# Loading three batches ahead of scales and weights, and the second half of batch 0 ahead of batch 2's statistics

## The chip, the cores and the metric

The kernel runs on one core of one Trainium2 chip. The metric is the device time of one execution in microseconds (us), as the median of several runs. TensorE (PE) does the matmuls and transposes, VectorE (DVE), ScalarE (ACT) and GpSimd (POOL) the elementwise work. SyncE (SP) issues nearly all loads and stores of the stretch that is changed here.

## The reference

For 16 batches of a 128x1024 tile `x` and a 128x256 tile `ctx`: a layer norm, a cross attention with a skip path, a second layer norm and a feed-forward network with 4-bit weights.

```python
n = layernorm(x)                                   # rows of 1024
q, k, v = Wq @ n, Wk @ ctx, Wv @ ctx
energy = einsum('bcn,bcm->bnm', q, k) / sqrt(C)    # C = 128
x = x + Wskip @ n + einsum('bnm,bcm->bcn', softmax(energy), v)
n = layernorm(x)
h = silu(n @ dequantize(gate).T) * (n @ dequantize(up).T)
x = x + h @ dequantize(down).T                     # inter = 2752, groups of 64
```

## The kernel before, in words

The work has two stages. The attention stage (the first 230 us or so) takes the 16 batches in `STEPS = 17` steps, one batch to a step, and writes the split, transposed activations to `xt`. The feed-forward stage that follows is a long run of matmuls (10 pairs of weight tiles in a hardware loop, and a remainder), for which DVE and ACT unpack the weights.

Each engine has its own program written out by hand, and each works strictly in the order of that program. Semaphores are the only tie between engines. So the order of the calls in `step(i)` of ACT, in `step(i, meanwhile)` of DVE and in SyncE's list of loads is the order in which things happen.

One batch is worked on in two halves, `f = 0` and `f = 1`, of 512 of the 1024 columns:

- DVE computes mean and variance of the batch's rows (`row_stats`: `BN_STATS` twice, `BN_AGGR` once), POOL makes the inverse deviation (`inverse_deviation`), DVE writes the normalised rows (`normalize(0, b)`, into `xn`).
- PE multiplies ctx by the fused query-key matrix and the value matrix (`keys_values(b)`, semaphore `s_kv`). ACT copies the keys to `kk` (`keys_out`) and the values to `v_t` (`values_out`).
- PE computes the energies of a half (`energies(b, f)`), DVE their row maxima (`maxima(b, f)`), ACT the exponentials with their sums (`exponentials`), DVE the inverse of the sums (`inverse_total`), ACT the scaled probabilities (`normalize_probs`). PE transposes them (`probs_transposed`), ACT copies them out (`probs_out`), PE multiplies by the values (`values(b, f)`), and DVE adds the result to the batch's row (`add_attention`).

In step `i` PE does `energies(i, 0)`, `values(i-1, 0)`, `energies(i, 1)`, `probs_transposed(i-1, 1)`, `keys_values(i+1)`, `values(i-1, 1)`, `probs_transposed(i, 0)`, with transposes of the second layer norm's blocks between them. `energies(i, 0)` needs `kk` of batch i, which ACT writes in step i-1.

SyncE's list in `before` begins with ctx and x of batches 0 and 1, then the six arrays of scales and zeros for all weights (172 KB each; DVE's `extremes` takes their maxima at the end of step 0, POOL reduces them over the partitions, and `powers_of_two` uses that in step 2), then the packed weights and the scale grid of the first weight tile (`load_raw(0, 0)`, `load_grid(0, 0)`; used from step 4 on), and then, for each further batch, its ctx and x. A load of batch i >= 2 waits for `s_kv >= i-1`, since ctx has two buffers; from batch 5 on it waits for the store of batch i-5 too.

In `before`, DVE's step 0 reads (L1056 is `inverse_total`, L1019 and L1023 are `row_stats`, L1041 is `maxima`, L981 is `extremes`):

```python
maxima(0, 0); inverse_total(0, 0)
x_arrived(2); row_stats(0, 2)      # waits for x of batch 2
maxima(0, 1)
extremes()                         # waits for scales and zeros
inverse_total(0, 1)
```

ACT's step 0 is `exponentials(0, 0)`, `normalize_probs(0, 0)`, `exponentials(0, 1)`, `keys_out(1)`, `normalize_probs(0, 1)`, `values_out(1)`, `probs_out(0, 0)`; L706 is an exponential, L720 a `normalize_probs`, L691 `keys_out`, L695 `values_out`, L701 `probs_out`. On PE L434 is `energies`, L422 `probs_transposed`, L462 and L467 are the skip part and the value part of `values`.

Of the kernel before, what the change touches and what calls it, by code (L numbers as in the profile page):

```python
# [15 lines left out]
B, C, N = 16, 128, 1024  # L16
# [29 lines left out]
def batch_of(i):  # L46

    return 8 * (i // 8) + i % 8 // 2 + 4 * (i % 2)
# [39 lines left out]
def build(nc, x, ctx_in, att_weights, packed, grids, scales, zeros, out):  # L88
    ctx = ExitStack()
    with ctx:  # L90
# [3 lines left out]
        def sem(name):  # L94
            return ctx.enter_context(nc.semaphore(name))
# [19 lines left out]
        grids_all = w_gu0[:, :, :, :].rearrange("p a o n -> p (a o n)")[:, 0:12 * 344].bitcast(F32).rearrange(  # L115
            "p (k n) -> p k n", k=6)
# [45 lines left out]
        s_grids_in = sem("s_grids_in")  # L162
# [75 lines left out]
        def wait(eng, s, count):  # L238
            if not isinstance(count, int) or count > 0:
                eng.wait_ge(s, count)  # L240

        @block.sync
        def _(sp):
            def load_batch(i):
                k, par = i // 2, i % 2
                if i >= 2:
                    sp.wait_ge(s_x_in[par], 16 * k)
                    wait(sp, s_kv, i - 1)
                if i >= XROWS:
                    sp.wait_ge(s_xn2, i - XROWS + 1)  # L250
                    sp.wait_ge(s_store[i % XROWS], 16 * (i // XROWS))
                b = batch_of(i)
                sp.dma_start(ctx_sb[:, par, :], ctx_in[b, :, :]).then_inc(s_ctx_in[par], 16)
                sp.dma_start(row(i), x[b, :, :]).then_inc(s_x_in[par], 16)

            def store_batch(i):
                sp.wait_ge(s_res, 2 * i + 2)
                sp.dma_start(out[batch_of(i), :, :], row(i)).then_inc(s_store[i % XROWS], 16)

            def load_grid(job, done):  # L260
                wait(sp, s_weight, done)
                for g in range(QG):
                    rows = slice(g * P // QG, (g + 1) * P // QG)
                    sp.dma_start(grid[rows, :, :], grids[job, g:g + 1, :, :].to_broadcast([P // QG, 2, JW])
                                 ).then_inc(s_grid_in, 16)

            def load_raw(job, done):
                wait(sp, s_weight_lo, done)
                sp.dma_start(raw[:, :], packed[job, :, :]).then_inc(s_raw_in, 16)

            def load_raw_d(job, done):
                wait(sp, s_weight_lo, done)
                sp.dma_start(raw_d[:, :], packed[job, :, :]).then_inc(s_raw_d_in, 16)

            load_batch(0)
            load_batch(1)
            for k in range(3):
                sp.dma_start(grids_all[:, k, :], scales[k, :, :]).then_inc(s_grids_in, 16)
                sp.dma_start(grids_all[:, 3 + k, :], zeros[k, :, :]).then_inc(s_grids_in, 16)
            load_raw(0, 0)  # L280
            load_grid(0, 0)
            for i in range(2, B):
                load_batch(i)
                if i >= 4:
                    store_batch(i - 4)
            store_batch(B - 4)
            store_batch(B - 3)
            load_raw(1, 4)
            load_grid(1, 2)
            store_batch(B - 2)  # L290
            store_batch(B - 1)

            def load_pair(p, base_lo, base_weight):
                if not isinstance(p, int):
                    load_raw(3 * p + 1, base_lo + 4)
                    load_grid(3 * p + 1, base_weight + 2)
                if isinstance(p, int):
                    sp.wait_ge(s_att, 2 * B)
                load_raw_d(3 * p + 2, base_lo)
                load_grid(3 * p + 2, base_weight + 4)  # L300
                load_raw(3 * p + 3, base_lo + 8)
                load_grid(3 * p + 3, base_weight + 6)

            load_pair(0, 0, 0)
            with sp.Fori(1, PAIRS, 1) as p:
                load_pair(p, 10 * p, 6 * p)
            load_raw(3 * PAIRS + 1, 10 * PAIRS + 4)
            load_grid(3 * PAIRS + 1, 6 * PAIRS + 2)
            load_raw_d(3 * PAIRS + 2, 10 * PAIRS)
            load_grid(3 * PAIRS + 2, 6 * PAIRS + 4)  # L310
            sp.wait_ge(s_nibble, 6 * PAIRS + 5)
            load_raw_d(3 * PAIRS + 3, 0)
            load_grid(3 * PAIRS + 3, 6 * PAIRS + 5)
            sp.wait_ge(s_p3, 4 * PAIRS + 2)
            for t in range(B):
                sp.wait_ge(s_acc[t % STAGES], 16 * (B // STAGES * (PAIRS - 1) + t // STAGES + 1))
                sp.dma_start(acc(t), out[t, :, :]).then_inc(s_acc_in[t], 16)
            for t in range(B):
                sp.wait_ge(s_last, 2 * t + 2)
                sp.dma_start(out[t, :, :], acc(t)).then_inc(s_out, 16)  # L320
            sp.wait_ge(s_out, 16 * B)
            for n in range(STAGES):
                sp.wait_ge(s_acc[n], 16 * (B // STAGES * PAIRS))
            for n in range(XROWS):
                sp.wait_ge(s_store[n], 16 * len(range(n, B, XROWS)))
# [358 lines left out]
        def _(act):  # L684
# [25 lines left out]
            def block_hi(unit):  # L710
                k, u = unit
                act.wait_ge(s_xt_ps, NTH_UNIT[unit] + 1)
                act.copy(xt[:, u, 0, :, P * k:P * k + P], ring_bank(("block", unit)).rearrange(  # L713
                    "p (j r) -> p j r", j=J)).then_inc(s_xt_hi, 1)
# [8 lines left out]
            def step(i):  # L723
                for unit in blocks_of_step(i, "sums"):
                    block_hi(unit)
                if i < B:
                    exponentials(i, 0)
                    normalize_probs(i, 0)
                for unit in blocks_of_step(i, "between"):
                    block_hi(unit)  # L730
                if i >= 1:
                    probs_out(i - 1, 1)
                if i % 2 == 0:
                    for unit in blocks_of_step(i, "after"):
                        block_hi(unit)
                if i < B:
                    exponentials(i, 1)
                if i % 2 == 1:
                    for unit in blocks_of_step(i, "after"):
                        block_hi(unit)  # L740
                if i + 1 < B:
                    keys_out(i + 1)
                if i < B:
                    normalize_probs(i, 1)
                if i + 1 < B:
                    values_out(i + 1)
                if i < B:
                    probs_out(i, 0)
# [228 lines left out]
        def _(dve):  # L977
# [58 lines left out]
            def x_arrived(i):  # L1036
                dve.wait_ge(s_x_in[i % 2], 16 * (i // 2) + 16)

            def maxima(b, f):
                dve.wait_ge(s_energy, 2 * b + f + 1)  # L1040
                dve.tensor_reduce(neg_max[:, f, :], ps_e[f], X_AXIS, ALU.max, negate=True).then_inc(s_max, 1)  # L1041
# [16 lines left out]
            def step(i, meanwhile=None):  # L1058
                if i < B:
                    maxima(i, 0)  # L1060
                for unit in blocks_of_step(i, "sums"):
                    block_lo(unit)
                if i >= 2:
                    normalize(1, i - 2)
                if i < B:
                    inverse_total(i, 0)
                if i >= 1:
                    add_attention(i - 1, 0)
                if i + 2 < B:
                    x_arrived(i + 2)  # L1070
                    row_stats(0, i + 2)
                if i < B:
                    maxima(i, 1)
                for unit in blocks_of_step(i, "between"):
                    block_lo(unit)
                if i % 2 == 0:
                    for unit in blocks_of_step(i, "after"):
                        block_lo(unit)
                if meanwhile:
                    meanwhile()  # L1080
                if i < B:
                    inverse_total(i, 1)
                if i % 2 == 1:
                    for unit in blocks_of_step(i, "after"):
                        block_lo(unit)
                if 1 <= i and i + 1 < B:
                    normalize(0, i + 1)
                if i >= 1:
                    add_attention(i - 1, 1)
                    dve.wait_ge(s_res, 2 * (i - 1) + 2)  # L1090
                    row_stats(1, i - 1)
# [397 lines left out]
```

## Time and profile before

| | |
|---|---|
| time, median of 3 runs | 1496.53 us (1495.29 to 1499.62) |
| the profiled execution, its own time | 1491.46 us |
| its span in the trace | 1489.7 us |
| busy time PE / DVE / ACT / POOL | 1454.0 / 820.4 / 634.3 / 206.6 us |
| bytes moved by DMA in the span | 174.82 MB |

The span runs from the first to the last recorded instruction. The profiled execution's own time holds 1.76 us around its span. Times in the trace count from the start of the span. Busy PE time includes matmuls that run back to back, so 98% busy does not say how fast they ran. The granted clock of TensorE is a separate column: 1.00 is 2.4 GHz, 0.50 is 1.2 GHz.

### The profile page before, as it was taken

What the parts mean: (1) busy time and instruction counts of PE and PEld (TensorE: products, weight loads), DVE (VectorE), ACT (ScalarE), POOL (GpSimd) and SP (SyncE); (2) the same over time, 40 slices, a digit from 0 to 9 for tenths busy, and PEclk for the clock granted to TensorE, in tenths of its full rate; (3) what the DMA queues carried; (4) which work ended last, traced back from release to release, by engine and by line L of the source; (5) the groups of instructions that cost most, each with busy time, mean ns of one, the idle gap of its engine ahead of it and who ended that gap; (6) DMA issues with size and microseconds to landing.
All of it is one profiled execution on the core that took longest, in us unless ns stands there. A gap on an engine that the chain in (4) does not pass through costs nothing.

```text
span 1489.7 us, 18688 instructions
## 1 busy us (share of the span) xinstructions
PE 1454.0 (98%) x6774; PEld 714.4 (48%) x6774; DVE 820.4 (55%) x1175; ACT 634.3 (43%) x1189; POOL 206.6 (14%) x265
## 2 busy tenths in 40 slices
PE   6999999999999999999999999999999999999998
PEld 5666765444444444444444444444444444444443
DVE  4888887744635544544554554554554463563265
ACT  5888893334244243333433333334333333433320
POOL 1233231011011011111101101101101101101100
PEclk9999999999999999999999999999999999999999
DMA  5222222157557547638638638637627637727794
GB/s 170 88 83 96 97 71 71 44 111 145 97 94 148 111 70 169 113 62 177 113 56 174 117 48 166 117 66 154 128 56 155 130 60 149 139 57 152 133 335 170
DMA packets 47028, 174.82 MB, mean 117 GB/s; under 512 B 6672, under 2 KB 9488, under 8 KB 42640
## 3 DMA queue, kind: packets, MB, share of 16 engines
q0 software_dynamic: 23040, 83.90, 33.1%
q1 hardware_dynamic: 23808, 90.20, 20.2%
q8 instruction: 20, 0.33, 0.1%
q10 hardware_dynamic: 144, 0.26, 0.0%
q14 instruction: 16, 0.13, 0.0%
HBM read 73.67 MB, written 100.66 MB: 117 GB/s over the span
## 4 chain that ended last, share of the span: by engine, by line
PE 90%; DVE 6%; issue 2%; ACT 2%; POOL 0%; ACTq 0%; DVEq 0%; POOLq 0%
PE ps L505 47%; PE ps L561 26%; PE ps L467 3%; PE ps L434 3%; PE ps L668 2%; PE ps L651 2%; PE ps L462 2%; PE ps L456 2%; PE ps L422 1%; DVE w_gu L1118 1%; DVE neg_max L1041 1%; ACT temps L706 1%; DVE quant L1134 0%; DVE quant L1129 0%; DVE raw L1127 0%
## 5 line engine op out<-in xcount | busy, mean ns | idle before, releaser
L505 PE MATMUL ps<-xt,w_gu 128*128 128x512 f16 x3528 | 789.2, 379 | 2.2 <-ACT temps L787 2.2
L505 PEld LDWEIGHTS ps<-xt,w_gu 128*128 128x128 f16 x3528 | 345.1, 98 | 417.4 <-ACT temps L787 3.0
L561 PE MATMUL ps<-w_d_all,h_all 128*128 128x512 f16 x1920 | 440.6, 379 | 5.6 <-ACT stage L817 5.6
L817 ACT ACTIVATE stage<-ps,pow 128x512 f32<-128x512 f32 x320 | 218.9, 687 | 390.5 <-PE ps L561 390.5
L561 PEld LDWEIGHTS ps<-w_d_all,h_all 128*128 128x128 f16 (+1 forms) x1920 | 187.1, 98 | 234.5 <-ACT stage L817 10.1
L382 POOL DMA_DIRECT2D out<-stage x160 | 138.6, 866 | 1039.1 <-ACT stage L817 1039.1
L1182 DVE TENSOR_TENSOR temps<-ps,temps 128x512 f32<-128x512 f32 x42 | 29.0, 691 | 236.1 <-PE ps L505 236.1
L804 ACT CAST h_all<-temps 128x512 f16<-128x512 f32 x42 | 25.8, 613 | 132.4 <-DVE temps L1201 132.4
L1187 DVE TENSOR_TENSOR temps<-ps,temps 128x512 f32<-128x512 f32 x42 | 29.0, 691 | 95.4 <-PE ps L505 95.4
L1191 DVE TENSOR_TENSOR temps<-ps,temps 128x512 f32<-128x512 f32 x42 | 28.9, 688 | 75.8 <-PE ps L505 75.8
L1195 DVE TENSOR_TENSOR temps<-ps,temps 128x512 f32<-128x512 f32 x42 | 28.9, 688 | 75.2 <-PE ps L505 75.2
L1178 DVE TENSOR_TENSOR temps<-ps,temps 128x512 f32<-128x512 f32 x42 | 29.0, 691 | 71.5 <-PE ps L505 71.5
L706 ACT ACTIVATE temps<-ps,neg_max 128x256 f32<-128x256 f32 x128 | 59.4, 489 | 12.3 <-DVE neg_max L1041 12.3
L792 ACT ACTIVATE temps<-ps,pow 128x512 f32<-128x512 f32 x42 | 28.9, 687 | 78.7 <-PE ps L505 78.7
L467 PE MATMUL ps<-temps,w_gu 128*128 128x512 f32 x128 | 60.1, 592 | 0.0
L720 ACT ACTIVATE temps<-temps,inv_total 128x256 f32<-128x256 f32 x128 | 54.7, 504 | 8.2 <-DVE inv_total L1056 8.1
L797 ACT ACTIVATE temps<-temps,pow 128x512 f32<-128x512 f32 x42 | 30.3, 721 | 54.6 <-DVE temps L1195 54.6
L1118 DVE TENSOR_TENSOR w_gu<-raw,w_gu 128x1024 f16<-128x1024 f32 (+1 forms) x43 | 52.9, 1231 | 0.0
L434 PE MATMUL ps<-w_gu,h_all 128*128 128x256 f32 x176 | 43.2, 391 | 6.1 <-ACT w_gu L691 4.4
L1046 DVE TENSOR_TENSOR xt<-ps,xt 128x512 f16<-128x512 f32 x56 | 37.1, 682 | 12.4 <-ACT xt L713 12.2
L1041 DVE TENSOR_REDUCE neg_max<-ps 128x4 f32<-128x1024 f32 x32 | 38.7, 1208 | 9.3 <-PE ps L434 8.9
L1113 DVE SCALAR_TENSOR_TENSOR quant<-quant,pow,grid 128x1024 f32<-128x1024 f32 (+1 forms) x34 | 43.3, 1274 | 0.1
(114 smaller groups left out, 1283.8 us busy)
## 6 DMA issues: line engine op xcount, KB each, us to landing
out<-stage POOLq DMA_DIRECT2D x160, 512.0 KB, 5.2
grid<-grids SPq DMA_DIRECT2D x136, 256.0 KB, 4.9
raw<-packed SPq DMA_DIRECT2D x22, 512.0 KB, 4.0
out<-stage SPq DMA_DIRECT2D x17, 512.0 KB, 2.6
stage<-x SPq DMA_DIRECT2D x13, 512.0 KB, 3.8
raw_d<-packed SPq DMA_DIRECT2D x12, 512.0 KB, 8.1
xt<-out SPq DMA_DIRECT2D x12, 512.0 KB, 10.7
out<-xt SPq DMA_DIRECT2D x12, 512.0 KB, 2.6
```

What stands on the lines that cost most here:

```text
L382: pool.dma_start(out[t, :, :], stage[:, t % STAGES, :], accum_op=ALU.add).then_inc(s_acc[t % STAGES], 16)
L434: mm = pe.matmul(ps_e[f][:, t, :], xn[b % XNS][:, cols], kk[:, par, :], start=True, stop=True)
L467: mm = pe.matmul(ps_o, v_t[:, par, h, :], prob_t[:, f, h, :], start=False, stop=(h == 1))
L505: mm = pe.matmul(bank, w_gu[e][:, wp, w, P * j:P * j + P], xt[:, xb, xp, j, cols], start=(fresh and n == 0), stop=(n == 3 * J - 1), skip_g ...
L561: mm = pe.matmul(ps[:, 6 + oh, :], h, w, start=(n == 0), stop=(n == len(products) - 1))
L706: ex = act.activation(prob[:, NTH * f + t, :], ps_e[f][:, t, :], ACT.Exp, bias=neg_max[:, f, t:t + 1], accum_out=total[:, f, t:t + 1])
L720: pn = act.activation(pr, pr, ACT.Copy, scale=inv_total[:, f, t:t + 1])
L817: act.activation(stage[:, t % STAGES, NOUT * oh:NOUT * oh + NOUT], ps[:, 6 + oh, :], ACT.Copy, scale=pow2[:, 10:11]).then_inc(s_stage, 1)
L1041: dve.tensor_reduce(neg_max[:, f, :], ps_e[f], X_AXIS, ALU.max, negate=True).then_inc(s_max, 1)
L1046: dve.tensor_tensor(xt[:, u, 1, :, P * k:P * k + P], ring_bank(("block", unit)).rearrange("p (j r) -> p j r", j=J), xt[:, u, 0, :, P * k:P ...
L1113: dve.scalar_tensor_tensor(out=t[:, cols], in0=t[:, cols], scalar=pow2[:, power:power + 1], in1=grid[:, 0, cols], op0=ALU.mult, op1=ALU.mu ...
L1118: dve.tensor_tensor(dst, src, hi, ALU.subtract).then_inc(s_weight_lo, 1)
```

## The change

SyncE's list is reordered: ctx and x of batch 2 are issued ahead of the scales and zeros, and the packed weights and grid of the first weight tile come after ctx and x of batch 4. In step 0 alone, DVE takes the maxima of the second half ahead of batch 2's statistics, and ACT copies the keys of batch 1 ahead of the second half's exponentials. Nothing is added or removed; every instruction of before is there once.

```diff
-            load_batch(0)
-            load_batch(1)
-            for k in range(3):
-                sp.dma_start(grids_all[:, k, :], scales[k, :, :]).then_inc(s_grids_in, 16)
-                sp.dma_start(grids_all[:, 3 + k, :], zeros[k, :, :]).then_inc(s_grids_in, 16)
-            load_raw(0, 0)
-            load_grid(0, 0)
-            for i in range(2, B):
+            for i in range(B):
                 load_batch(i)
+                if i == 2:
+                    for k in range(3):
+                        sp.dma_start(grids_all[:, k, :], scales[k, :, :]).then_inc(s_grids_in, 16)
+                        sp.dma_start(grids_all[:, 3 + k, :], zeros[k, :, :]).then_inc(s_grids_in, 16)
+                if i == 4:
+                    load_raw(0, 0)
+                    load_grid(0, 0)
                 if i >= 4:
                     store_batch(i - 4)
...
+                if i == 0:
+                    keys_out(1)
                 if i < B:
                     exponentials(i, 1)
...
-                if i + 1 < B:
+                if 0 < i < B - 1:
                     keys_out(i + 1)
...
                 if i + 2 < B:
+                    if i == 0:
+                        maxima(0, 1)
                     x_arrived(i + 2)
                     row_stats(0, i + 2)
-                if i < B:
+                if 0 < i < B:
                     maxima(i, 1)
```

The line numbers of ACT do not change ahead of `step`; those of DVE rise by two, so that `maxima` is L1041 before and L1043 after. PE's and POOL's programs are the same in both.

SyncE's queue, from the load of batch 1 to that of batch 3, before:

```order
L253 DMA w_gu<-ctx 128x256
L254 DMA stage<-x 128x1024
L278 DMA w_gu<-scales 128x344
L279 DMA w_gu<-zeros 128x344
...
L269 DMA raw<-packed 128x1024
L264 DMA grid<-grids 32x2048 x4
L253 DMA w_gu<-ctx 128x256 [waits s_kv,s_x_in0]
L254 DMA stage<-x 128x1024
L253 DMA w_gu<-ctx 128x256 [waits s_kv,s_x_in1]
L254 DMA stage<-x 128x1024
```

and after, on to the load of batch 4 and the first store (`out<-stage`); the `w_gu<-x` row is batch 4, whose row lies in memory that `w_gu1` takes later:

```order
L253 DMA w_gu<-ctx 128x256 [waits s_kv,s_x_in0]
L254 DMA stage<-x 128x1024
L279 DMA w_gu<-scales 128x344
L280 DMA w_gu<-zeros 128x344
...
L253 DMA w_gu<-ctx 128x256 [waits s_kv,s_x_in1]
L254 DMA stage<-x 128x1024
L253 DMA w_gu<-ctx 128x256 [waits s_kv,s_x_in0]
L254 DMA w_gu<-x 128x1024
L269 DMA raw<-packed 128x1024
L264 DMA grid<-grids 32x2048 x4
L258 DMA out<-stage 128x1024 [waits s_res]
```

The load of batch 2 now has nothing but batches 0 and 1 ahead of it, and the scales and zeros stand behind its wait for `s_kv`.

DVE in step 0, before:

```order
L1056 RECIPROCAL inv_total<-total 128x4 [waits s_exp]
L1014 MEMSET carrier 128x1 [waits s_x_in0]
L1019 BN_STATS stats<-stage 128x6 x2
L1014 MEMSET carrier 128x1 [waits s_stat1]
L1023 BN_AGGR mv<-stats 128x2
L1041 TENSOR_REDUCE neg_max<-ps 128x4 [waits s_energy]
L981 TENSOR_REDUCE pow<-w_gu 128x1 [waits s_grids_in]
```

and after:

```order
L1058 RECIPROCAL inv_total<-total 128x4 [waits s_exp]
L1043 TENSOR_REDUCE neg_max<-ps 128x4 [waits s_energy]
L1016 MEMSET carrier 128x1 [waits s_x_in0]
L1021 BN_STATS stats<-stage 128x6 x2
L1016 MEMSET carrier 128x1 [waits s_stat1]
L1025 BN_AGGR mv<-stats 128x2
L983 TENSOR_REDUCE pow<-w_gu 128x1 [waits s_grids_in]
```

The maxima of the second half moved from behind the wait for x of batch 2 to ahead of it.

ACT in step 0, before:

```order
L720 ACTIVATE temps<-temps,inv_total 128x256 x3
L706 ACTIVATE temps,total<-ps,neg_max 128x256 [waits s_max]
L706 ACTIVATE temps,total<-ps,neg_max 128x256 x3
L691 ACTIVATE w_gu<-ps 128x256 [waits s_kv]
L720 ACTIVATE temps<-temps,inv_total 128x256 [waits s_inv]
```

and after:

```order
L720 ACTIVATE temps<-temps,inv_total 128x256 x3
L691 ACTIVATE w_gu<-ps 128x256 [waits s_kv]
L706 ACTIVATE temps,total<-ps,neg_max 128x256 [waits s_max]
L706 ACTIVATE temps,total<-ps,neg_max 128x256 x3
L720 ACTIVATE temps<-temps,inv_total 128x256 [waits s_inv]
```

The copy of batch 1's keys (L691) moved ahead of four exponentials.

## Rows read from the trace of the kernel before

**Rows 1.** The page: busy time, and the chain that ended last by engine.

```profile
PE 1454.0 (98%) x6774; PEld 714.4 (48%) x6774; DVE 820.4 (55%) x1175; ACT 634.3 (43%) x1189; POOL 206.6 (14%) x265
PE 90%; DVE 6%; issue 2%; ACT 2%; POOL 0%; ACTq 0%; DVEq 0%; POOLq 0%
```

**Rows 2.** The chain that ended last, 0 to 90 us: start, duration, work.

```profile
15.30 2.40 issue
...
20.35 1.93 ACT temps L706 x8
...
22.61 3.45 PE ps L434 x8
...
35.59 1.98 PE ps L434 x8
```

**Rows 3.** Timeline of SyncE's queue: start, time to issue, transfer.

```profile
5.97 1.82 SPq L264 DMA_DIRECT2D grid<-grids  x4
...
8.40 0.45 SPq L254 DMA_DIRECT2D stage<-x  x1
...
32.56 0.43 SPq L254 DMA_DIRECT2D w_gu<-x  x1
36.12 0.34 SPq L258 DMA_DIRECT2D out<-stage  x1
...
44.91 0.43 SPq L254 DMA_DIRECT2D stage<-x  x1
```

**Rows 4.** Busy time by stretch; last three columns: granted clock, DMA share, GB/s.

```profile
2.00:10.50 8.50, 6.88 (x36) 6.30 (x37) 3.71 (x11) 1.37 (x4) 0.93 (x3) 1.00 1.01 380
10.50:15.50 5.00, 2.94 (x16) 2.46 (x14) 2.12 (x3) 2.09 (x9) 0.57 (x2) 1.00 1.02 220
15.50:18.50 3.00, 1.09 (x8) 0.86 (x8) 0.80 (x3) 1.54 (x4) 0.00 (x0) 1.00 1.01 376
18.80:25.50 6.70, 2.89 (x7) 2.36 (x8) 4.07 (x11) 4.76 (x16) 0.74 (x2) 0.50 0.00 0
```

**Rows 5.** Timeline of DVE: start, duration, work, idle time before it.

```profile
5.43 0.69 DVE L1019 BATCH_NORM_STATS2 stats<-stage 128x6 f32<-128x512 f32 x1 [5.43 <-issue]
...
15.13 0.18 DVE L1056 RECIPROCAL inv_total<-total 128x4 f32<-128x4 f32 x1 [2.00 <-ACT temps L706]
17.70 0.69 DVE L1019 BATCH_NORM_STATS2 stats<-stage 128x6 f32<-128x512 f32 x1 [2.40 <-issue]
...
19.15 1.17 DVE L1041 TENSOR_REDUCE neg_max<-ps 128x4 f32<-128x1024 f32 x1
20.23 2.59 DVE L981 TENSOR_REDUCE pow<-w_gu 128x1 f32<-128x344 f32 x6
22.74 0.17 DVE L1056 RECIPROCAL inv_total<-total 128x4 f32<-128x4 f32 x1
```

**Rows 6.** Timeline of ACT, same columns.

```profile
15.34 1.70 ACT L720 ACTIVATE temps<-temps,inv_total 128x256 f32<-128x256 f32 x4 [0.24 <-DVE inv_total L1056]
...
22.16 0.39 ACT L691 ACTIVATE w_gu<-ps 128x256 f32<-128x256 f32 x1
22.95 1.70 ACT L720 ACTIVATE temps<-temps,inv_total 128x256 f32<-128x256 f32 x4 [0.39 <-DVE inv_total L1056]
...
24.81 1.06 ACT L701 COPY temps<-ps 128x512 f32<-128x512 f32 x2
27.35 0.47 ACT L706 ACTIVATE temps<-ps,neg_max 128x256 f32<-128x256 f32 x1 [1.48 <-DVE neg_max L1041]
```

**Rows 7.** Timeline of PE, same columns.

```profile
17.10 1.09 PE L422 MATMUL ps<-ident,temps 128*128 128x128 f32 x8 [3.66 <-ACT temps L720]
...
26.75 1.88 PE L467 MATMUL ps<-temps,w_gu 128*128 128x512 f32 x4
28.47 1.89 PE L434 MATMUL ps<-w_gu,h_all 128*128 128x256 f32 x8
```

**Rows 8.** Timeline of POOL: the first instruction behind the reduction over partitions.

```profile
33.68 0.18 POOL L342 TENSOR_TENSOR var_eps<-mv,eps 128x1 f32<-128x1 f32 x1 [7.40 <-issue]
```

**Rows 9.** DMA issues up to 20 us: count, KB each, median us to landing.

```profile
grid<-grids SPq DMA_DIRECT2D x4, 256.0 KB, 7.7
```

## The prediction

> **What bounds the kernel now.** The page comes first: PE is busy for 98% of the span and carries 90% of the chain that ended last [rows 1]. So almost everywhere the end is set by PE's own sequence, and this change does not touch that sequence. A microsecond can be won only where PE stands idle on the chain. Taken in order of time, the chain shows such a place at the very start: DVE waits 2.40 us from 15.30, ACT's exponentials of batch 0's second half run at 20.35, and PE takes up batch 1's energies only at 22.61; from there the chain stays on PE until batch 2's energies at 35.59 [rows 2]. The change aims at 15 to 23 us. Whatever it wins there must still be there at 35.59, and then it goes through to the end, since nothing later waits for the clock on the wall: all later loads are issued on semaphores that work of the same stage raises.
>
> **What the 2.40 us are.** DVE's statistics of batch 2 begin at 17.70 behind an idle 2.40 that no engine ended [rows 5]; what is left is x of batch 2, issued at 8.40 [rows 3]. If SyncE's queue is served in order, ahead of it and with it go 256 KB of attention weights, batches 0 and 1 (1280 KB), scales and zeros (1032), the packed weights (512), the grid (1024) and batch 2 itself (640): 4744 KB, or 4858 thousand bytes. The stretches moved 8.5 x 380 + 5.0 x 220 = 4330 thousand by 15.5, and the rest at 376 takes 1.4 us more, so 16.9 [rows 4]. With 0.8 us for the landing that is the 17.70 seen. So batch 2 was late because of what was ahead of it, not because of its own issue.
>
> **The loads in the new order.** Batch 2 still waits for batch 0's x and for the first keys; it can be issued at about 7.7 and 8.2 instead of 8.40, which is no gain in itself. But only batches 0 and 1 are ahead: 1536 KB, gone by 2.0 + 1573/380 = 6.1. Its 640 KB need 1.7 us at 380, so it lands at 8.2 + 1.7 + 0.8 = 10.7; I take 12 with a margin. Scales and zeros are six issues of 0.46 us (1.82 for four in [rows 3]) from about 8.6, the last at about 11, and 1057 thousand bytes take 2.8 us: landed by 15. The load of batch 3 keeps its place, as it waits for batch 1's keys at 13.4 in both.
>
> **DVE, start to start** [rows 5]. Inverse of half 0 at 15.13. The maxima of half 1 follow at 15.23 (before: 19.15) and hold DVE for 1.08 (19.15 to 20.23). Batch 2's statistics at 16.31 find their x landed; 1.45 (17.70 to 19.15) gives 17.76. The six reductions of scales and zeros find them landed since 15; 2.51 (20.23 to 22.74) gives the inverse of half 1 at 20.27 instead of 22.74: **2.47 us** earlier.
>
> **ACT** [rows 6]. Probabilities of half 0 at 15.34; four take 1.60 start to start. Keys of batch 1 then go at 16.95 (before: 22.16) and cost 0.36, all of it now ahead of the exponentials: 17.31 instead of 20.35. They take 1.93 [rows 2] and end at 19.25, so the 0.36 cost nothing: ACT then waits for DVE until 20.27. That is the new wait, 1.0 us, behind the reductions. From there probabilities, values and the copies of the transposed probabilities move with the 2.47: the copies at 22.34 instead of 24.81, over at 23.40. Exponentials of batch 1 can start at 23.35, if their maxima are there.
>
> **PE** [rows 7]. The transposes at 17.10 stay. Behind them batch 1's energies need the keys (17.31 + 0.03), so they run at about 18.0, not at 22.61. Here a second gain shows. Before, PE had idled 4.4 us when they began, the granted clock was 0.50 from 18.8 to 25.5 [rows 4], and the eight matmuls took 3.45 us, against 1.98 for the same eight at 35.59 [rows 2]. Without that 1.47 the value matmuls could have begun with their input at 25.37 (24.81 + 0.56, half of the copies), not at 26.75: the slow clock cost 1.38. Now the energies are done by 20 to 21.5 even if slow, their maxima by 22.7, ahead of ACT's 23.35. The value matmuls start on their copies at 22.34 + 0.56 = 22.9 instead of 26.75: **3.85 us** earlier. On ACT the exponentials of batch 1 start 27.35 - 23.35 = 4.0 earlier. PE's path from the values to 35.59 has no other wait in it, so batch 2's energies come at 31.8: the smaller of the two, **3.8 us**.
>
> **What could cost something behind that.** POOL's reduction ends at 33.68 before [rows 8], 10.9 us after DVE's maxima of the scales; now about 31.2. Should it end at 33.68 all the same, rows of batch 1's second norm would wait some 0.5 us on a DVE that idles more than that. I take 0. The packed weights and the grid now go out behind batch 4, at about 29 instead of 5.5, and need five issues (2.3 us) and 1.6 MB, 1.4 us at 376 and 5 us at 220: until about 38. The first store, issued at 36.12 before and at 32.3 now, is behind them and lands near 40; batch 5's load, which waits for it, was at 44.91 and is wanted at 41.1 [rows 3]. It could slip by a microsecond, and its x is read ten later. 0 again. The weights are first touched in step 4, 30 us on.
>
> **The sum.** The profiled execution took 1491.46 us (its span 1489.7 and 1.76 around it); by the sum it would take 1487.7. The median of the unprofiled runs is 5.1 above it, a difference that no row explains; I put the 3.8 against the median: 1496.53 - 3.8 = **1492.7 us**, or 0.25% less. A change of less than 0.3% (4.5 us) is what this kernel's measurement hardly tells from none.
>
> **The rivals.**
>
> Rival 1, the clock takes its part back. PE now idles twice: 3.66 before the transposes, as before [rows 7], and from about 20.9 (energies and the skip part done) to 22.9. In the trace the clock fell at 18.8, after a stretch in which PE was busy for 1.09 of 3.00 us, and rose at about 25.5, 2.9 us after PE had resumed [rows 4]. If it falls near 21 now, the values (1.88) and energies (1.89 [rows 7]) of the next stretch run at half speed for as long, and lose 1.45: gain 2.4, time 1494.1. For it: two short gaps. Against it: PE is busy for 2.8 of the 3.8 us from 17.1, more than in the stretch before the fall. The Trainium skill, in "TensorE: Matmul & The Clock Gate", Part 1, says that the gate's monitor does not start anew with the kernel, so that the point of a change varies from run to run. By that rule some runs would show this rival and others not; one trace cannot tell.
>
> Rival 2, more than the sum. x of batch 0 is what DVE waits for until 5.43 [rows 5], at a time when scales were in the queue; with the engines freed it may land up to 0.7 us sooner (0.3 MB beyond what stood ahead of it had moved, at 380), and before's slow clock may last longer in other runs than in the trace: gain 4.5 to 5.5, time 1491.5.
>
> Rival 3, the order of the queue is not the reason, and batch 2 still lands at 17.6. Then the maxima are ahead anyway, statistics at 17.70, reductions at 19.15, inverse at 21.66: 1.1 on ACT, and 1.4 of clock: gain 2.4, 1494.1. The bytes above speak against it.
>
> Rival 4, slower: scales and zeros, now behind a wait on SyncE, land late and hold the reductions, and with them the inverse, ACT and PE. They cost nothing until 17.76. With the grid's 7.7 us [rows 9] from 11.1 they land at 18.8 and cost 1.0. They eat the whole gain at 21.6, and the kernel is slower by 0.3% if they land at 26.1, 15 us after issue, about twice the longest time to landing in these rows: 1501.
>
> **Chances.** The sum 0.50, rival 1 0.22, rival 2 0.15, rival 3 0.05, rival 4 or a like delay that ends slower 0.05; 0.03 for what I don't see. Faster by over 0.3%: nearly all of rival 2, and a quarter of the sum's cases by scatter (the three runs lie 4.3 us apart): 0.27. Slower 0.04. Within 0.3%: 0.69. The range takes in the gains from 1.0 to 5.5 with about a microsecond of scatter: 1489.5 to 1495.8.
>
> **What would show it.** Right: no idle time before batch 2's statistics, which start near 16.3; inverse of half 1 near 20.3, straight behind the reductions; keys of batch 1 near 17; batch 1's energies near 18, batch 2's near 31.8. Wrong: a clock of 0.50 at 21 to 26 (rival 1); statistics at 17.7 still (rival 3); idle time before the reductions (rival 4); the first statistics well before 5.43 (rival 2); or batch 2's energies near 31.8 but the feed-forward stage no earlier than before, which would mean a wait later on that my reading has missed.

## The result, and the profile after

The changed kernel takes 1488.6 us in the median of 6 runs (1487.43 to 1489.89), against 1496.39 for the kernel before (6 runs, 1493.27 to 1499.62). The ratio is 0.995, with a 95% interval of 0.9938 to 0.9961: 7.8 us less, where 3.8 were forecast. The two profiled executions, though, are only 3.7 us apart (1491.46 and 1487.79 us), and their spans 4.1 (1489.7 and 1485.6). So the trace gave what was forecast, and as much again came in executions that were not read. Two executions among those of the experiments below, of 1549.62 and 5496.44 us, stand far from all others and count in no ratio and no span.

The queue of SyncE after (start, time to issue, transfer), for [rows 3]:

```profile
7.90 0.43 SPq L254 DMA_DIRECT2D stage<-x  x1
...
10.75 0.43 SPq L280 DMA_DIRECT2D w_gu<-zeros  x1
...
29.21 0.43 SPq L269 DMA_DIRECT2D raw<-packed  x1
29.69 1.84 SPq L264 DMA_DIRECT2D grid<-grids  x4
31.86 0.36 SPq L258 DMA_DIRECT2D out<-stage  x1
...
40.84 0.43 SPq L254 DMA_DIRECT2D stage<-x  x1
```

x of batch 2 is issued at 7.90 instead of 8.40, with nothing but batches 0 and 1 ahead. The first store and batch 5 follow at 31.86 and 40.84, forecast at 32.3 and 41.1: the loads that were put between did not hold them up.

DVE's timeline after, for [rows 5]:

```profile
5.25 0.69 DVE L1021 BATCH_NORM_STATS2 stats<-stage 128x6 f32<-128x512 f32 x1 [5.25 <-issue]
...
15.04 1.20 DVE L1043 TENSOR_REDUCE neg_max<-ps 128x4 f32<-128x1024 f32 x1
16.16 0.69 DVE L1021 BATCH_NORM_STATS2 stats<-stage 128x6 f32<-128x512 f32 x1
...
17.61 2.55 DVE L983 TENSOR_REDUCE pow<-w_gu 128x1 f32<-128x344 f32 x6
20.07 0.17 DVE L1058 RECIPROCAL inv_total<-total 128x4 f32<-128x4 f32 x1
```

The idle 2.40 us ahead of batch 2's statistics are gone, and the inverse of half 1 stands directly behind the reductions, at 20.07 (22.74 before; 20.27 forecast).

ACT and PE after, for [rows 6, 7]:

```profile
16.77 0.36 ACT L691 ACTIVATE w_gu<-ps 128x256 f32<-128x256 f32 x1
...
22.14 1.06 ACT L701 COPY temps<-ps 128x512 f32<-128x512 f32 x2
23.09 0.49 ACT L706 ACTIVATE temps<-ps,neg_max 128x256 f32<-128x256 f32 x1
```

```profile
17.85 1.89 PE L434 MATMUL ps<-w_gu,h_all 128*128 128x256 f32 x8
...
22.86 1.96 PE L467 MATMUL ps<-temps,w_gu 128*128 128x512 f32 x4 [2.26 <-ACT temps L701]
...
31.58 1.89 PE L434 MATMUL ps<-w_gu,raw_d 128*128 128x256 f32 x8
```

Batch 1's energies run at 17.85 in 1.89 us (22.61 and 3.45 before), the values of batch 0 at 22.86 (26.75), and batch 2's energies at 31.58 (35.59, forecast 31.8). The granted clock, third from the end in the first row below, stayed at 1.00 where it had been 0.50 [rows 4]:

```profile
18.80:25.50 6.70, 4.44 (x15) 2.49 (x14) 2.98 (x8) 5.13 (x18) 0.40 (x1) 1.00 0.01 2
```

### The profile page after: what moved, and what is told of

Read it like the earlier page. It is cut to its first block, busy times and chain, and to the rows that moved or that the text cites. A ratio compares the mean times of both kernels' runs of the same rounds, so it can differ in the third digit from the quotient of the medians.

```text
span 1485.6 us, 18688 instructions
## 1 busy us (share of the span) xinstructions
PE 1452.2 (98%) x6774; PEld 712.9 (48%) x6774; DVE 820.5 (55%) x1175; ACT 634.1 (43%) x1189; POOL 206.6 (14%) x265
## 4 chain that ended last, share of the span: by engine, by line
PE 90%; DVE 6%; issue 2%; ACT 2%; POOL 0%; ACTq 0%; DVEq 0%; POOLq 0%
PE ps L505 47%; PE ps L561 26%; PE ps L467 3%; PE ps L434 3%; PE ps L668 2%; PE ps L651 2%; PE ps L456 2%; PE ps L462 2%; PE ps L422 1%; DVE w_gu L1122 1%; DVE neg_max L1043 1%; DVE quant L1138 0%; DVE quant L1133 0%; DVE raw L1131 0%; PE ps L410 0%
## 5 line engine op out<-in xcount | busy, mean ns | idle before, releaser
L1043 DVE TENSOR_REDUCE neg_max<-ps 128x4 f32<-128x1024 f32 x32 | 38.7, 1209 | 6.2 <-PE ps L434 5.7
```

## The experiments

Medians below are of the device time. A ratio is to the kernel before measured side by side with the kernel in question, with its 95% interval behind it; it is not exactly the quotient of the two medians. Beside it stand the lowest and the highest span among all executions of the kernel, since the scatter tells as much as the median here. The widths of two such ranges are only roughly comparable, since more executions spread further. When x of a batch had landed is read from the start of DVE's statistics of it, which is the latest it can have been.

### The kernel before once more

No edit. The question was in which executions the other 4 us lie, and where.

> The kernel before, unchanged, for a second trace. The shown trace of before took 1491.5 us where the median is 1496.4; the changed kernel took 1487.8 with its trace and 1488.6 in the median. So 3.8 of the 7.8 us are in the traces and 4 are not. Theory A (the clock): most executions of before have TensorE at 1.2 GHz longer, or in one more place, than the trace that was read; this trace shows more than the 6.7 us at 0.50, all of it at 15 to 35 us. Theory B (the loads): in most executions x of batch 2 lands some 4 us later than 17.6; this trace shows batch 2's statistics near 21 to 22. Theory C (elsewhere): batch 2's energies start at 35 to 36 us again and the time is lost later on.

Measured: 1496.94 us (10 runs), ratio 1.0007 (0.9995 to 1.0019). This trace has a span of 1496.3 us, 6.6 more than the one that was read. Its chain:

```profile
15.38 0.18 DVE inv_total L1056
15.56 6.23 issue
...
26.70 3.78 PE ps L434 x8
...
40.81 1.74 PE ps L434 x8
```

The wait for x of batch 2 is 6.23 us instead of 2.40 [rows 2], and batch 2's energies come at 40.81 instead of 35.59. That is theory B. The stretches show how the loading ends (granted clock, DMA share, GB/s at the end of each row):

```profile
18.50:19.50 1.00, 0.00 (x0) 0.00 (x0) 0.00 (x0) 0.00 (x0) 0.00 (x0) 0.50 0.84 316
20.00:23.00 3.00, 0.00 (x0) 0.00 (x0) 1.21 (x3) 0.00 (x0) 0.00 (x0) 0.50 0.06 25
25.50:32.00 6.50, 5.30 (x11) 3.56 (x12) 2.72 (x6) 4.29 (x13) 0.40 (x1) 0.50 0.00 0
```

Up to 19.5 nearly all DMA engines are busy. From 20 to 23 the share is 0.06, one sixteenth, at 25 GB/s: as much as a single one of the 16 engines gives, still working off its part of the queue. The Trainium skill ("DMA: Bandwidth & Descriptors", "Why a DMA increments its semaphore by 16 and not by 1") says that the engines of one DMA finish independently and that only the full count of the semaphore means that all data has landed. The trace agrees: DVE's wait for x of batch 2 ends at 21.79, within this stretch. In the trace that was read first there was no such tail, the share is 0.00 from 18.8 on [rows 4].

The tail is not all. The loads as a whole were slower too, as 15 to 17 us shows in four traces with the old queue. From top to bottom they are the first trace of before (batch 2's statistics at 17.70), this one (21.79), that of the order alone (18.93) and that of before with PE kept busy (22.07); the columns are the stretch, its length, granted clock, DMA share and GB/s:

```profile
15.00:17.00 2.00, 1.00 1.01 324
15.00:17.00 2.00, 1.00 0.97 226
15.00:17.00 2.00, 0.72 0.99 239
15.00:17.00 2.00, 1.00 1.01 180
```

The DMA engines are equally busy in all four, and in the last three they move less. By the bytes moved in each stretch, the 4858 thousand of the prediction were through at about 16.9, 17.8, 17.6 and 18.7 (an estimate, since the trace does not tell whose bytes they are). So of the 4.1 us by which x of batch 2 is later here, some 0.9 is the whole queue and some 3 the tail.

The clock is a further, smaller part: PE idled 8 us here, and the clock stayed at 0.50 up to 32, so that the skip part (1.69 us) ran slow too.

In four series the kernel before was executed 96 times beside other kernels. Its spans go from 1490.4 to 1497.5, with a median of 1493.7. The trace on which the forecast stood, 1489.7, is below every one of them.

### The load order alone

```diff
...
-            for i in range(2, B):
+            for i in range(B):
                 load_batch(i)
+                if i == 2:
+                    for k in range(3):
...
+                if i == 4:
+                    load_raw(0, 0)
+                    load_grid(0, 0)
```

> Only the order of SyncE's queue is changed; DVE and ACT keep the old order. By durations of the traces: x of batch 2 landed by 12, statistics at 15.2, maxima of half 1 at 16.7, exponentials 17.9 to 19.8, keys at 19.8, batch 1's energies at 20.2, inverse of half 1 at 20.3, batch 2's energies near 31.8. Theory A (clock): PE idles about 2 us here instead of 4.4, so most of the whole gain, 5.5 to 8 us, 1489 to 1491. Theory B (loads): the same, since the late load is gone, 7 to 8 us. If neither holds and only the trace's own 3.8 are there, 1492.6.

Measured: 1491.65 us, ratio 0.9975 (0.9965 to 0.9985), spans 1487.0 to 1490.0. This is 4.4 us of the 7.8, less than either theory gave it (5.5 to 8 and 7 to 8). Its trace has batch 2's statistics directly behind the inverse of half 0, at 15.02, as expected, but batch 1's energies at 19.93 took 3.52 us at the slow clock and are on the chain, so that batch 2's come at 32.99 and not at 31.8. The late load is gone with this edit, the clock's part is not.

### The order on DVE and ACT alone

The edits of `step` are those of the change; SyncE's queue is that of before.

> Only the order on DVE (maxima of half 1 ahead of the statistics of batch 2) and on ACT (keys of batch 1 ahead of the exponentials) is changed; SyncE's queue is that of before. Statistics of batch 2 still at 17.7, inverse of half 1 at 21.7, batch 1's energies near 18.0, values of batch 0 near 24.3, batch 2's energies near 33.2. Theory A (clock): PE's idle time is split in two as in the changed kernel, so all that the clock cost comes back: 2.4 + 4 = 6 us, 1490. Theory B (loads): the late load still holds DVE, only the 1.1 of the order and 1.4 of clock come back: 1494.

Measured: 1493.44 us, ratio 0.9986 (0.9975 to 0.9996), 2.6 us less; spans 1487.5 to 1494.1. The median is near theory B's number (1494). The spans stay 6.6 us apart, as those of before (7.1), where the load order alone brought them to 3.0: the scatter comes with the loads and not with the order.

The trace, however, is not the one that was expected. x of batch 2 came at 18.93 and not at 17.7:

```profile
18.93 0.69 DVE L1021 BATCH_NORM_STATS2 stats<-stage 128x6 f32<-128x512 f32 x1 [2.56 <-issue]
```

Batch 1's energies at 18.82 and the values of batch 0 at 25.63 ran at the slow clock (3.62 and 3.26 us), and batch 2's energies came at 36.05 instead of 33.2, later than in the first trace of before (35.59). So two short gaps did not keep the clock up in this execution, and of what the median's 2.6 us are made is not shown.

### The kernel before with PE kept busy

```diff
                 if i < B:
                     probs_transposed(i, 0)
+                if i == 0:
+                    for _ in range(FILL):
+                        pe.matmul(ps_o[:, 0:P], ident[:, :], ident[:, :], start=True, stop=True)
```

`FILL` is 10.

> The kernel before with ten matmuls of the identity (results not used) on PE between the transposes of batch 0 and the energies of batch 1, so that PE is busy through most of the idle time at 18.2 to 22.6. Nothing else is changed. In the trace read before, the slow clock cost 1.4 us. Theory A (clock): 1.4 to 5.5 us faster, 1491 to 1495, and the runs lie closer together than the 6 us of before. Theory B (loads): at most 1.4 faster, and the scatter stays.

Measured: 1495.46 us, ratio 0.9993 (0.9979 to 1.0007), spans 1490.3 to 1497.3. The median is 0.6 us lower, and the interval reaches from 3.1 us faster to 1.0 slower: the upper part of theory A is out, its 1.4 us are not excluded. The scatter stays, as theory B has it. The trace (span 1496.4) has batch 2's statistics late again; the fillers ended at 22.6, the energies came 4.4 us later and ran slow all the same:

```profile
22.07 0.69 DVE L1023 BATCH_NORM_STATS2 stats<-stage 128x6 f32<-128x512 f32 x1 [6.24 <-issue]
```

```profile
26.97 3.78 PE L435 MATMUL ps<-w_gu,h_all 128*128 128x256 f32 x8 [4.39 <-ACT w_gu L695]
```

So this kernel did not take the slow clock away where the load was late, and it tests theory A only where it was early. What it shows is that x of batch 2 can be late with PE kept busy up to 22.6.

### Which load lags: only packed weights and grid moved

```diff
-            load_raw(0, 0)
-            load_grid(0, 0)
             for i in range(2, B):
                 load_batch(i)
+                if i == 4:
+                    load_raw(0, 0)
+                    load_grid(0, 0)
```

> The kernel before with one part of the load order changed: packed weights and grid of the first tile go behind batch 4; scales and zeros stay ahead of batch 2. DVE and ACT as before. The first call showed that x of batch 2 lands anywhere from 17.7 to 21.8 us with the old queue, and that the last of it comes over one sixteenth of the DMA engines' share, 25 GB/s. Theory L (an engine that lags on the grid's loads): the grid is what has to go; batch 2 lands by 12, its statistics follow the inverse of half 0 at 15.0, and this kernel is as fast and as close together as the one with both moved: 1491.7, 1489 to 1493. Theory Q (any bytes ahead count): 2.6 MB instead of 4.2 are ahead, and the time lies between, 1493.

Measured: 1491.19 us, ratio 0.9977 (0.9968 to 0.9986), spans 1487.1 to 1490.1. That is as fast and as close together as with both moved, and batch 2's statistics are at 15.41 in the trace: theory L. The interval alone would just leave room for theory Q's 1493.

### Only scales and zeros moved

```diff
-            for k in range(3):
...
             load_raw(0, 0)
             load_grid(0, 0)
             for i in range(2, B):
                 load_batch(i)
+                if i == 2:
+                    for k in range(3):
...
```

> The kernel before with the other part changed: scales and zeros go behind batch 2; packed weights and grid stay ahead of it. DVE and ACT as before. By the rates of the first trace x of batch 2 lands at 14.8, which would cost nothing, and scales and zeros at 18. Theory L: the lag of up to 4 us comes with the grid's loads and is still ahead of batch 2; it lands between 15 and 19, and the runs scatter by 5 us or more around 1492.5 to 1494.5. Theory Q: 3.1 MB are ahead instead of 4.2; the runs are as close as with both moved, near 1492.

Measured: 1493.11 us, ratio 0.9986 (0.9975 to 0.9996), spans 1488.1 to 1493.6. Slower than the last and nearly twice as wide (5.5 us instead of 3.0), with fewer bytes taken from the queue (1.0 MB instead of 1.6): theory L again, though this comparison alone would fit theory Q's count of bytes too. In the trace x of batch 2 came at 16.18, at the early end of what was expected:

```profile
16.18 0.69 DVE L1020 BATCH_NORM_STATS2 stats<-stage 128x6 f32<-128x512 f32 x1 [0.93 <-issue]
```

### Only the grid moved

```diff
             load_raw(0, 0)
-            load_grid(0, 0)
             for i in range(2, B):
                 load_batch(i)
+                if i == 4:
+                    load_grid(0, 0)
```

> The kernel before with nothing but the four loads of the first grid moved behind batch 4; scales, zeros and packed weights stay ahead of batch 2. Theory L (the lag comes with the grid's loads): 1491.2 to 1491.7 as with grid and packed weights moved, spans 1487 to 1490. Theory R (any of the loads lags, the packed weights too): between that and before, near 1493, spans over 4 us or more.

Measured: 1491.48 us, ratio 0.9965 (0.9953 to 0.9977), spans 1487.0 to 1490.6. The median is 4.7 us below that of before, against 4.4 and 4.2 where more was moved: as far as these medians tell, the four grid loads alone account for all that the new load order brings to the kernel before. This is also the answer to theory Q. The grid is 1024 KB, scales and zeros are 1032 KB, and moving those brought 2.3 us and left the spans 5.5 apart. The trace:

```profile
15.27 0.69 DVE L1020 BATCH_NORM_STATS2 stats<-stage 128x6 f32<-128x512 f32 x1
```

The slow stretch of the DMA goes with these loads as well. From 11 to 13 us the first row is the kernel before, the second this one:

```profile
11.00:13.00 2.00, 1.00 0.97 209
11.00:13.00 2.00, 1.00 0.87 345
```

### The changed kernel with the grid back ahead of batch 2

```diff
+                if i == 2:
+                    load_raw(0, 0)
+                    load_grid(0, 0)
                 load_batch(i)
...
-                if i == 4:
-                    load_raw(0, 0)
-                    load_grid(0, 0)
```

> The changed kernel with packed weights and grid of the first tile put back ahead of batch 2; scales and zeros stay behind batch 2, and DVE and ACT keep the new order. If the grid's loads hold batch 2 back and by a different amount each time, x of batch 2 lands between 15 and 19 (16.2 with the same queue in an earlier trace), which is free until 16.2 here and costs one for one beyond; scales and zeros land 2 to 3 us behind it and hold the reductions. Spans from 1486 to 1491 where the changed kernel's are 1485.5 to 1487.7, median 1490.5. If the order on DVE and ACT covers it all, 1488.6.

Measured: 1491.9 us (1488.47 to 1498.97), ratio 0.9981 (0.9966 to 0.9996), spans 1486.3 to 1496.1. With packed weights and grid back, the median is 3.3 us above the changed kernel's first 1488.6 (3.8 us below before instead of 7.8; by the ratio 2.8), and the spans, 9.8 us apart, scatter more than those of before beside it (6.3) and far more than expected (1486 to 1491). The trace is one of the early cases (span 1486.5), so what the late ones wait for was not read; even here the reductions now wait for the zeros that were queued behind the grid:

```profile
18.51 2.60 DVE L983 TENSOR_REDUCE pow<-w_gu 128x1 f32<-128x344 f32 x6 [0.96 <-DMA w_gu<-zeros]
```

### The changed kernel once more

> The changed kernel, unchanged, on the same chip as the others of this call. 1488.6; batch 2's statistics at 16.2 as in its first trace, and spans in two groups, near 1485.6 and 1487.3, which differ by a clock that falls near 257 us or not. If its landing scattered too, the spans would be spread over 4 us as those of before are.

Measured: 1489.17 us, ratio 0.9956 (0.994 to 0.9971). Batch 2's statistics at 16.35, and the 12 spans of both series in two groups, 1485.5 to 1486.0 and 1487.1 to 1487.7. This trace is of the second group. The first row below is from it, the second from the trace shown above:

```profile
260.00:264.00 4.00, 4.00 (x13) 1.45 (x11) 3.88 (x5) 1.30 (x2) 0.00 (x0) 0.60 0.01 4
```

```profile
260.00:270.00 10.00, 10.00 (x49) 4.48 (x47) 9.18 (x13) 1.30 (x2) 0.00 (x0) 1.00 0.16 55
```

Near 257 us PE idles 2.2 us until ACT has copied a product (L789), which stands behind ACT's casts of weights, and the clock falls behind it in some executions (0.60 over 4 us) and not in others. The two traces are 0.2 us apart at batch 2's energies (31.93 and 31.74 in the chain) and 1.9 at the end, so this fall costs 1.7. More traces say the same, as far as nothing else differs in them. From batch 2's energies to the end it is 1454.0 to 1454.1 us in the five where the clock stayed at 1.00 there (the first traces of before and after, load order alone, order alone, grid back), and 1455.6 to 1455.7 in the five where it fell (only scales moved, grid and packed weights moved, only grid moved, this one, and the next one below). The same trace had a low clock at the beginning as well:

```profile
17.00:23.00 6.00, 5.36 (x18) 4.00 (x18) 4.61 (x12) 4.67 (x17) 0.74 (x2) 0.72 0.02 8
```

That one cost nothing (batch 2's energies are as far behind the inverse of half 0 in both traces, 16.8 us), since batch 1's energies are not on the chain any more.

### The changed kernel with PE kept busy

```diff
+                if i == 1:
+                    fill(4)
                 if i >= 1:
                     values(i - 1, 0)
...
+                if i == 0:
+                    fill(8)
                 if i < B:
                     probs_transposed(i, 0)
```

`fill(n)` is n matmuls of the identity into `ps_o`, not used.

> The changed kernel with matmuls of the identity on PE, their results not used: eight ahead of the transposes of batch 0 (idle 3.7 us) and four ahead of the values of batch 0 (idle 2.3 us). The changed kernel's trace had a clock of 1.00 throughout and 1485.6 us; others of its executions had a mean clock of 0.998 and 1487.2 to 1487.4. If the clock's fall at these two gaps is what makes them longer, they go: all executions near 1487.5 and 0.8 us less in the median. If the fall comes in another place, near 262 us, where PE waits for the weights, nothing changes.

Measured: 1488.95 us (5 runs), ratio 0.9958 (0.9945 to 0.9971), spans 1485.6 to 1487.5 in the same two groups. The clock at 13 to 25.5 was 1.00, and at 258 to 262 it was 0.64 in a trace of 1487.1:

```profile
258.00:262.00 4.00, 3.85 (x12) 1.50 (x13) 3.30 (x5) 1.21 (x3) 0.00 (x0) 0.64 0.00 0
```

The clock's fall at the first gaps has no price that these runs show in the changed kernel; the two groups come from the later place.

### The reductions a step later

```diff
-            step(0, extremes)
+            step(0)
...
                 if i < B:
                     maxima(i, 0)
+                if i == 1:
+                    extremes()
...
-                2: powers_of_two,
+                3: powers_of_two,
```

POOL's reduction goes behind `inverse_deviation(1, 0)` in its step 1.

> The changed kernel with the six reductions of scales and zeros moved out of step 0 on DVE: they stand behind the maxima of batch 1 in step 1, POOL's reduction over the partitions behind its two inverse deviations of step 1, and the use of the result in step 3. In the changed kernel's trace the inverse of half 1 stands behind the reductions at 20.1 while its exponentials end at 18.9. With them gone it can go at 18.9: 1.1 us earlier, and so all that follows. 1487.5 against 1488.6. If a new wait takes it (POOL late for batch 1's second norm or batch 3), 1488.6 or more.

Measured: 1491.52 us, ratio 0.9973 (0.9963 to 0.9983): 2.9 us slower than the changed kernel's 1488.6, which was not measured beside it. The inverse came at 19.07 as expected, but POOL's reduction ended only near 49, 14 us behind the instruction ahead of it, and DVE waited for the inverse deviation behind it:

```profile
49.13 0.18 POOL L342 TENSOR_TENSOR var_eps<-mv,eps 128x1 f32<-128x1 f32 x1 [7.78 <-issue]
```

```profile
50.82 0.81 DVE L1036 TENSOR_SCALAR h_all<-stage,mv,rstd 128x1024 f32<-128x1024 f32 x1 [3.16 <-POOL rstd L345]
```

That is not the whole price: PE idled longer behind this wait, and from 56 to 60 us the clock was 0.58, where the changed kernel's trace has 1.00. How the 2.9 us divide was not measured.

### The reductions behind the inverse

```diff
-            step(0, extremes)
+            step(0)
+            extremes()
```

> The changed kernel with one line moved: DVE's six reductions of scales and zeros stand behind the inverse of half 1 of batch 0 instead of ahead of it, still ahead of batch 1's maxima. In the changed kernel's trace that inverse starts at 20.1 while its exponentials end at 18.9. The inverse then starts at 19.0, the copies at 21.0, the values of batch 0 at 21.8 (now 22.9); batch 1's maxima come at 21.6 to 22.7 and hold ACT's exponentials to 22.8 (now 23.1). Batch 2's energies 0.8 us earlier. POOL's reduction begins 1.5 later than now, and batch 1's second norm waits some 1.2 us for it, under idle time of DVE. 1487.8, against 1488.6. If POOL's delay is not covered: 1488.6 or more, as where the reductions were put a step later, which cost 2.9.

Measured: 1488.56 us against 1489.17 for the changed kernel beside it; ratios 0.9952 (0.9936 to 0.9968) and 0.9956. Batch 2's energies are at 30.88 in the chain, against 31.93, of which 0.35 was there at the inverse of half 0 (14.78 and 15.13), so 0.7 us as expected. POOL's delay was covered: PE's last matmuls end at 1482.48 against 1483.31, so the lead is still there. Both traces end at 1487.5 all the same, since what follows DVE's last instruction took 4.3 us here and 3.4 there. The median's 0.6 cannot be told from nothing with six runs each, and the fastest spans are alike (1485.4 and 1485.5). It is not shown to beat the changed kernel.

## Why the prediction was wrong

**What bounds it, and where the gain lies: right.** Each instant of the sum stood in the trace within 0.25 us: statistics 16.16 (16.31), inverse 20.07 (20.27), batch 1's energies 17.85 (18.0), values 22.86 (22.9), batch 2's energies 31.58 (31.8). The clock's part, 1.4 us, was there too. What was won at 31.6 reached the end: 4.0 and 4.1 us.

**The step that failed: "What the 2.40 us are", as a size.** The cause was right, the queue ahead of batch 2. But the sum of bytes at mean rates gave one landing time, 16.9 + 0.8, and the wait was entered as 2.40 us. The 0.8 stands on no row: it is what made the sum meet the one trace, so that the agreement tested nothing. The second trace has 6.23 us, the filled kernel 6.24. Two things were taken for fixed there that are not: the rate, which was 180 to 324 GB/s over the same two microseconds in four traces, and the landing behind the last bytes, 0.8 us in one trace and, by the same estimate, 4.0 in the second. That this is what the new load order removes is shown by the edits: with the grid's four loads moved, the spans of the kernel before shrink from 7.1 us to 3.6 and the median falls by 4.7 us; with grid and packed weights put back into the changed kernel the spans widen from 2.2 us to 9.8.

**"A difference that no row explains; I put the 3.8 against the median": the second half of the same error.** Most of the 5.1 us between the profiled execution and the median were this: 4.0 of them lie within the span (1489.7 against a median of 1493.7). The trace was the fastest case of a kernel that scatters, and the change removes the scatter, so the gain in the median was larger than that between the two traces. The 3.8 us were put in as if the typical execution waited as briefly as the fastest. The three runs given, 4.3 us apart, and the 5.1 us were the warning. Nor is a change of 0.3% out of reach of the measurement, as the forecast had it: six runs of each kernel gave the ratio to within 0.12% either way.

**Rival 1, the clock takes its part back: wrong** where it was placed. The clock did fall in one execution (0.72 at 17 to 23), at no cost. The fall that costs 1.7 us is near 257 us, which the forecast did not look at. Against this rival the forecast counted PE busy for 2.8 of the 3.8 us from 17.1; by its own durations, and in the trace after, PE has no idle time there at all until its skip part is done. **Rival 2, more than the sum: right in sign, too small, and only its lesser cause was there.** x of batch 0 landed only 0.2 us sooner (5.25). The slow clock of before does last longer in the second trace (to 32), but there PE had idled 8.26 us behind the late load instead of 4.42, and this rival did not name the load. **Rival 3** is refuted by the traces: with the new queue the statistics of batch 2 have no idle time before them. **Rival 4**, late scales, did not come; it shows in small, 0.96 us, once packed weights and grid are ahead of them.

**How the parts add.** Loads alone 4.4 us, order alone 2.6, both 7.8 in the first series and 7.0 in the second: within the scatter, the sum of the two.

**Open.** Why one DMA engine lags with the grid's loads in the queue, and by how much in which execution, is not settled; nor why the engines move less while they are as busy. Those four loads each go to 32 partitions and read one row of 8 KB for all 32, unlike all others on this queue here; no kernel varied that. How much of the median's 7.8 us is landing and how much clock was not separated: two traces of before give 4.1 us of landing (17.70 and 21.79), 5.2 at batch 2's energies, and 6.6 at the end, the last 1.4 about the size of the later fall (the clock is 0.63 at 268 to 272 in the second trace). In the changed kernel 5 of 12 spans seem to have that fall; how often it comes in the kernel before is not known.

## What to carry to other kernels

Compare the profiled execution with the other runs before making a sum from it: where it is faster than all of them, some wait in it may be an early case, and a wait on a load is a good first suspect. A load that the start depends on should have nothing ahead of it in its queue that is not needed sooner, and what is to be asked is not when the bytes are through but when the slowest DMA engine is. A change that shields the chain from a scattering load is worth more in the median than the trace of an early case shows. Here moving four loads alone brought 4.7 us in the median.

## What was not expected of the hardware

A load behind a full queue landed between 17.7 and 22.1 us in traces of kernels with the same queue (17.70, 18.93, 21.79 and 22.07). In the trace with 21.79 the last 3 us ran at 25 GB/s and a DMA share of 0.06. With 1.6 MB of grid and packed weights taken out of its way the spans of the same kernel stay within 3.0 us.

GpSimd's reduction over partitions of a 128x6 tile occupies its queue for 10.3 to 13.8 us in four traces, though the row of it shows 0.40. The reductions on DVE end at 20.1 in the changed kernel, and this is what GpSimd has from there on:

```profile
24.28 0.40 POOL L364 PARTITION_ALL_REDUCE pow_tmp<-pow  x1 [5.63 <-issue]
31.74 0.18 POOL L342 TENSOR_TENSOR var_eps<-mv,eps 128x1 f32<-128x1 f32 x1 [7.07 <-issue]
```

The same idle time of TensorE is followed by either clock: behind 3.7 us ahead of the transposes of batch 0, these took 1.09 us in the first trace of the changed kernel and 1.97 in that of the load order alone.
